# Expert chunks of a two-expert router: rows sent to one list, handed on to the other list, stored once

## The chip, the cores and the metric

The kernel runs on one core of a Trainium2 chip. The metric is the device time of one execution in microseconds (us); before the change three timed runs gave 500.67, 501.40 and 501.75, median 501.4. A core has TensorE (PE; its weight loads are shown apart as PEld), VectorE (DVE), ScalarE (ACT), GpSimd (POOL) and SyncE (SP), which run their own instruction streams and meet at semaphores, and 16 DMA engines that they share.

## The reference

3125 tokens (graph nodes) of 256 numbers pass one layer:

```python
xn = _layernorm(x)
x = x + _L0_gnn_ref(xn, src, dst, ...) + _L0_mix_ref(xn[None], ...)[0]
x = x + _L0_ffn_ref(_layernorm(x)[None], ...)[0]

# _L0_ffn_ref, with tokens = _layernorm(x), 8 experts, the best 2 of each token:
rw, re = jax.lax.top_k(softmax(tokens @ router_w.T), 2)
rw = rw / rw.sum(-1, keepdims=True)
combine = zeros((N, E)).at[arange(N)[:, None], re].set(rw)
out = tokens
for e in range(8):
    y = gelu(tokens @ w1[e] + b1[e]) @ w2[e] + b2[e]
    out = out + combine[:, e:e + 1] * y
```

The first line's two terms are a graph network over 53125 edges and a linear attention. The change lies in the last one. For these inputs the best expert (rank 0) is chosen by 248, 448, 389, 253, 479, 398, 435 and 475 tokens, the second (rank 1) by 270, 403, 411, 291, 488, 389, 433 and 440. In chunks of 128 rows of one expert that makes 28 chunks of rank 0 and 30 of rank 1.

## The kernel before

The graph and attention stages run until about 280 us. Tokens lie 125 to a partition in 25 tiles, `rows[125, 25, ROW]`; a row holds the 256 normalized numbers (`xb`) and 5 more: the token's number, the weights of rank 0 and rank 1, and the spread and mean with which the un-normalized value is restored.

*Routing.* The 25 tiles are taken in six groups (`ROUT`: 2, 5, 5, 5, 5, 3 tiles). For a group ScalarE normalizes, TensorE transposes and makes the logits, VectorE picks the two experts (`choose`), weighs and works out the place of each token in the lists (`weigh`, line 1051). `slot_i` (line 1067) holds for each token two row numbers in the DRAM tensor `xs`: one in the list of its rank 0 expert, one in that of its rank 1 expert. `xs` has two halves of RR rows, one for each rank. When a group's slots are there, GpSimd sends its rows to the rank 0 lists, one indirect DMA a tile (`send`, line 543: 125 rows of 1044 bytes). Rank 1 sends of earlier tiles are put between: one behind each of the groups 0 to 4, eight behind group 5 (BETWEEN, EARLY), and the last 12 between the chunks.

*The chunk table.* VectorE counts the lists and makes a table of 2 x 32 chunks (lines 1087 to 1120): expert and first row of each. A list whose length isn't a multiple of 128 is filled at its front with null rows, and the chunks behind the last real one read null rows only. A null row has the token number NOWHERE, so that its scatter is out of bounds and moves nothing. The null rows are written early by SyncE: two large stores (line 357) and 16 small ones (line 392), one behind each of 16 transposing DMAs of the graph stage.

*The chunks.* Chunks 0 to 31 are rank 0, 32 to 63 rank 1, and all engines run through them as one loop. For each, SyncE loads 128 rows from `xs` into `xch` (six buffers; `load_chunk`, line 394; buffer c % 6 is free when VectorE has weighed chunk c - 6). TensorE transposes them (`turn_rows`), does the first layer (line 1466) and the second (lines 1475 and 1477); it runs `turn_rows(c+2)`, `first_layer(c+1)`, `second_layer(c)` in this order. ScalarE copies the transposed rows, does the gelu and, for rank 0, restores the un-normalized rows in place (`restore`, line 709). VectorE copies the expert's weights two chunks ahead (lines 1129, 1130) and then weighs (`weigh_rows`): for rank 0 weight x y + restored row (line 1142), for rank 1 weight x y (line 1145), into one of four buffers `ys`. GpSimd scatters `ys` to the tokens' rows of `out` (`add_rows`, line 555): rank 0 by a plain write, rank 1 by an accumulating one, behind a wait for all rank 0 writes. SyncE waits for the rank 0 sends before chunk 0 and for the rank 1 sends before chunk 32. Ahead of chunk 0 TensorE runs 20 matmuls that only keep it busy (`keep_clock`, line 1165).

## Time and profile before

| | |
|---|---|
| timed runs | 500.67, 501.40, 501.75 us; median 501.4 |
| span of the profiled execution, first to last instruction | 511.2 us |
| PE busy | 456.7 us, 89% of the span |
| DVE, ACT, POOL busy | 318.7, 288.5, 234.0 us |
| graph and attention | 0 to about 280 us |
| routing | about 280 to 344 us |
| chunks | 356 to 504 us |
| chain that ended last | PE 57%, POOL 11%, issue 11%, DMA 8%, DVE 6% |

The profiled execution has no time of its own beside its span; the span is 9.8 us longer than the median of the timed runs. Times of rows are us from the span's start. "Issue" is a wait for which the profile shows no cause. A group of matmuls shows the time from its first start to its last modelled end. A gap in square brackets is idle time of the engine ahead of the instruction, with what ended it.

### The profile page before, as it was taken

How to read it: one execution, taken by the hardware profiler on the slowest of the kernel's cores; microseconds unless marked ns; L12 is line 12 of the kernel's file. 1: busy time of each engine (PE TensorE's matmuls, PEld its weight loads, DVE VectorE, ACT ScalarE, POOL GpSimd, SP SyncE). 2: the span in 40 equal slices, each digit the busy share in tenths (PEclk: the TensorE clock that was granted, in tenths of full speed). 3: DMA queues.
4: the chain of work that ended last, by engine and by line, in shares of the span. 5: the costliest groups of instructions: out<-in, count | busy, mean ns of one | idle time of the engine just before them, and what ended most of it. 6: DMA issues, size and time to landing. Idle time of an engine off the chain costs nothing.

```text
span 511.2 us, 10298 instructions
## 1 busy us (share of the span) xinstructions
PE 456.7 (89%) x3383; PEld 341.3 (67%) x3383; DVE 318.7 (62%) x866; ACT 288.5 (56%) x657; POOL 234.0 (46%) x259
## 2 busy tenths in 40 slices
PE   2899999978999999999998999735979889999994
PEld 1788888855666665566554575522968778999993
DVE  3686658755777776777740898472356466666662
ACT  1775555556777776777761688500556556544441
POOL 5035865453111111111110027778557765688775
PEclk9999999997999999999998998767899999999999
DMA  8705310947667776677662012334434444367763
GB/s 219 171 3 166 84 24 4 316 96 144 150 149 150 151 150 151 151 150 130 130 134 60 3 32 77 83 89 116 129 105 136 132 122 123 74 112 119 115 109 36
DMA packets 122451, 58.73 MB, mean 115 GB/s; under 512 B 95797, under 2 KB 119585, under 8 KB 122398
## 3 DMA queue, kind: packets, MB, share of 16 engines
q1 hardware_dynamic: 107838, 42.83, 35.8%
q0 software_dynamic: 13744, 14.39, 13.2%
q10 hardware_dynamic: 816, 0.85, 0.7%
q8 instruction: 28, 0.46, 0.4%
q14 instruction: 25, 0.20, 0.1%
HBM read 19.14 MB, written 20.34 MB: 77 GB/s over the span
## 4 chain that ended last, share of the span: by engine, by line
PE 57%; POOL 11%; issue 11%; DMA 8%; DVE 6%; ACT 4%; SPq 1%; POOLq 1%; DVEq 0%; another core or an unknown queue 0%; ACTq 0%
PE bank L1265 11%; PE bank L1254 9%; POOL out L562 6%; PE bank L1466 6%; POOL xs L544 5%; PE bank L1477 4%; PE bank L1190 4%; DMA region_a<-region_a 4%; PE bank L1296 4%; PE bank L1200 3%; PE bank L1203 3%; DMA rows<-in_x 2%; PE bank L1165 2%; PE bank L1276 2%; PE bank L1455 1%
## 5 line engine op out<-in xcount | busy, mean ns | idle before, releaser
L628 ACT CAST region_a<-bank 128x500 bf16<-128x500 f32 (+1 forms) x175 | 111.6, 667 | 48.6 <-PE bank L1254 43.0
L544 POOL DMA_INDIRECT xs<-rows,slot_i x50 | 62.5, 1249 | 50.3 <-issue 45.1
L1265 PE MATMUL bank<-region_a,region_z 125*64 125x500 bf16 (+1 forms) x525 | 72.1, 371 | 3.2 <-DMA region_a<-region_a 3.2
L1466 PE MATMUL bank<-region_a,region_c 128*128 128x128 f32 x512 | 70.7, 282 | 4.8 <-ACT region_a L697 2.6
L1254 PEld LDWEIGHTS bank<-region_a 128*128 128x128 bf16 x625 | 41.2, 102 | 46.1 <-issue 32.0
L518 POOL COPY wide<-den 125x256 f32<-125x256 f32 x25 | 11.4, 455 | 127.3 <-DVE den L942 127.3
L1254 PE MATMUL bank<-region_a 128*128 128x125 bf16 x625 | 65.4, 223 | 4.0 <-ACT region_a L628 2.8
L1466 PEld LDWEIGHTS bank<-region_a,region_c 128*128 128x128 f32 x512 | 63.8, 196 | 7.3 <-issue 3.6
L1477 PE MATMUL bank<-region_c,region_a 128*128 128x256 f32 x256 | 66.1, 380 | 0.0
L705 ACT ACTIVATE region_a<-bank,region_c 128x128 f32<-128x128 f32 x128 | 40.2, 366 | 42.9 <-PE bank L1466 24.9
L562 POOL DMA_INDIRECT out<-region_a x32 | 53.1, 1661 | 14.3 <-issue 12.3
L1129 DVE COPY region_c<-region_w 128x1026 f32 x64 | 46.2, 722 | 20.5 <-issue 20.3
L697 ACT COPY region_a<-bank 128x256 f32<-128x256 f32 x64 | 23.9, 374 | 44.6 <-PE bank L1455 39.9
L1477 PEld LDWEIGHTS bank<-region_c,region_a 128*128 128x128 f32 x256 | 44.1, 192 | 4.2
L866 DVE TENSOR_TENSOR region_a<-iota,locs 128x3200 bf16<-128x3200 bf16 x25 | 46.2, 1848 | 0.0
L559 POOL DMA_INDIRECT out<-region_a x32 | 33.8, 1057 | 25.9 <-DVE region_a L1142 19.1
L860 DVE TENSOR_TENSOR region_a<-iota,keys 128x3150 bf16<-128x3150 bf16 x25 | 45.4, 1818 | 0.2 <-PE bank L1254 0.2
L1140 DVE CAST region_a<-region_a 128x1 int32<-128x1 f32 x64 | 9.9, 155 | 49.8 <-issue 32.6
L1265 PEld LDWEIGHTS bank<-region_a,region_z 125*64 125x64 bf16 x525 | 25.0, 111 | 23.3 <-DMA region_a<-region_a 3.9
L1165 PE MATMUL bank<-zeros,ones 128*128 128x512 bf16 x114 | 32.9, 437 | 6.8 <-DVE expert_i L1119 6.8
L467 POOL TENSOR_SCALAR rows<-rows,rstd,shift 125x256 f32<-125x256 f32 x25 | 18.2, 732 | 33.1 <-DVE region_a L753 33.0
L1190 PE MATMUL bank<-wzkv,region_a 128*125 128x320 f32 x100 | 32.3, 446 | 0.0
(219 smaller groups left out, 800.3 us busy)
## 6 DMA issues: line engine op xcount, KB each, us to landing
region_a<-xs SPq DMA_DIRECT2D x64, 130.5 KB
region_w<-in_w SPq DMA_DIRECT2D x4, 1024.0 KB, 9.4
rows<-in_x SPq DMA_DIRECT2D x5, 560.0 KB
xs<-null SPq DMA_DIRECT2D x16, 130.5 KB, 2.3
xs<-null SPq DMA_DIRECT2D x2, 913.5 KB, 7.7
ztab<-region_z SPq DMA_DIRECT2D x5, 234.4 KB
out<-region_a POOLq DMA_INDIRECT x64
xs<-rows,slot_i POOLq DMA_INDIRECT x50
```

The costliest lines, as they stand in the source:

```text
L544: nc.gpsimd.indirect_dma_start(xs, bass.IndirectOffsetOnAxis(slot_i[:, t, r2:r2 + 1], 0), rows[:, t, :], None).then_inc(sent[r2], 16)
L562: nc.gpsimd.indirect_dma_start(out, to, ys[:, c % 4, :], None, bounds_check=N - 1, oob_is_err=False, compute_op=ALU.add).then_inc(added[c ...
L628: nc.scalar.copy(to, chunk_ps[n % 2][:, 0:w * TP].rearrange("p (c t u) -> p c t u", c=w, t=NT)).then_inc(adj_done, 1)
L860: nc.vector.tensor_tensor(koh[:, t % 2, :, :].rearrange("p c (m u) -> p c m u", u=2), counting(KW), columns(keys, t, KW), ALU.is_equal).th ...
L866: nc.vector.tensor_tensor(loh[:, t % 2, :, :].rearrange("p c (m u) -> p c m u", u=2), counting(P), columns(locs, t, P), ALU.is_equal).then ...
L1129: nc.vector.tensor_copy(wc[:, c % 3, :].rearrange("p (a f) -> p a f", a=1), w_all[:, bass.ds(e, 1), :])
L1165: nc.tensor.matmul(ps[:], ones16[:], zeros[:], start=True, stop=True)
L1190: last = nc.tensor.matmul((y0, y1)[s][0:TP, 0:H1 + D], xnT[:, s, k, :], wzkv[:, k, 0:H1 + D], start=(k == 0), stop=(k == 1))
L1254: last = nc.tensor.matmul(chunk_ps[n % 2][:, (c - lo) * TP:(c - lo + 1) * TP], loh[:, t % 2, c, :], koh[:, t % 2, c, 0:TP], start=True, st ...
L1265: last = nc.tensor.matmul(block_out(b), zparts[:, t, part, :], adjT[0:TP, t % 2, lo:hi, 0:TP], start=False, stop=False, skip_group_check=True)
L1466: last = nc.tensor.matmul(hid_ps[c % 2][:, f * P:(f + 1) * P], wc[:, c % 3, k * D + f * P:k * D + (f + 1) * P], xT[:, c % 2, k * P:(k + 1) ...
L1477: last = nc.tensor.matmul(y_ps[c % 2][:, 0:D], hT[:, c % 2, f * P:(f + 1) * P], wc[:, c % 3, (2 + f) * D:(3 + f) * D], start=False, stop=( ...
```

## The change

A token's row is sent once, to its rank 0 list. It carries its row number in the rank 1 list as a sixth extra number (NEXT, from `slot_f`), so ROW is 262. `xs` has one half; a second DRAM tensor `xs_next` holds the rank 1 lists with rows of WIDE = ROW + 256 numbers (2072 bytes). A rank 0 chunk is loaded into the front part of a buffer of `xch` (now 8 buffers, WIDE each); ScalarE writes the restored row to the back part (PART), VectorE adds weight x y there, and GpSimd scatters the whole wide row to `xs_next` (`hand_on`). SyncE waits until all 32 of these scatters have landed, then loads rank 1 chunks with wide rows; VectorE adds weight x y to the part, and GpSimd writes it to `out` by a plain scatter (`write_rows`). A buffer is free when its scatter has landed (`added`). The loops of TensorE and ScalarE no longer run through the border between chunk 31 and 32, and TensorE runs 20 more `keep_clock` matmuls there. The null rows of `xs_next` are wide. The 25 rank 1 sends and the buffers `ys` are gone.

```diff
-ROW = D + 5
+ROW = D + 6
+PART, WIDE = ROW, ROW + D
+TOKEN, NEXT, W_A, W_B, SPAN, MEAN = range(D, D + 6)
...
-BETWEEN, EARLY = 1, 13
-XB = 6
+XB = 8
...
-    xs = nc.dram_tensor("xs", (2 * RR, ROW), F32, kind="Internal").ap()
+    xs = nc.dram_tensor("xs", (RR, ROW), F32, kind="Internal").ap()
+    xs_next = nc.dram_tensor("xs_next", (RR, WIDE), F32, kind="Internal").ap()
...
-            for r2 in range(2):
-                sp.dma_start(xs[r2 * RR + NX * CAP:(r2 + 1) * RR, :].rearrange("(b p) d -> p b d", p=P),
-                             null[:].rearrange("p (a d) -> p a d", a=1).to_broadcast([P, NULLS, ROW])
+            for to, w in ((xs, ROW), (xs_next, WIDE)):
+                sp.dma_start(to[NX * CAP:RR, :].rearrange("(b p) d -> p b d", p=P),
+                             null[:, 0:w].rearrange("p (a d) -> p a d", a=1).to_broadcast([P, NULLS, w])
                              ).then_inc(nulls_stored, 16)
...
                     r2, e = divmod(t - 2, NX)
-                    at = r2 * RR + e * CAP
-                    sp.dma_start(xs[at:at + P, :], null[:]).then_inc(nulls_stored, 16)
+                    to, w = ((xs, ROW), (xs_next, WIDE))[r2]
+                    sp.dma_start(to[e * CAP:e * CAP + P, :], null[:, 0:w]).then_inc(nulls_stored, 16)
...
                 if c >= XB:
-                    sp.wait_ge(ys_done, c - XB + 1)
-                sp.dma_start(xch[:, c % XB, :], xs[bass.ds(at, P), :]).then_inc(xch_in[c % XB], 16)
+                    sp.wait_ge(added[c % XB], c // XB * 16)
+                if c < MC:
+                    sp.dma_start(xch[:, c % XB, 0:ROW], xs[bass.ds(at, P), :]).then_inc(xch_in[c % XB], 16)
+                else:
+                    sp.dma_start(xch[:, c % XB, :], xs_next[bass.ds(at, P), :]).then_inc(xch_in[c % XB], 16)
...
-            sp.wait_ge(sent[0], NT * 16)
+            sp.wait_ge(sent, NT * 16)
             for c in range(NCH):
                 if c == MC:
-                    sp.wait_ge(sent[1], NT * 16)
+                    for s in range(XB):
+                        sp.wait_ge(added[s], len(range(s, MC, XB)) * 16)
                 load_chunk(c)
...
                 for t in range(lo, hi):
-                    send(t, 0)
-                for t in range(g * BETWEEN, (g + 1) * BETWEEN if g < NR - 1 else EARLY):
-                    send(t, 1)
+                    send(t)
...
+            def hand_on(c):
                 pool.wait_ge(ys_done, c + 1)
+                nc.gpsimd.indirect_dma_start(xs_next, bass.IndirectOffsetOnAxis(to_row[:, c:c + 1], 0),
+                                             xch[:, c % XB, :], None, bounds_check=RR - 1, oob_is_err=False
+                                             ).then_inc(added[c % XB], 16)
+
+            def write_rows(c):
+                pool.wait_ge(ys_done, c + 1)
+                nc.gpsimd.indirect_dma_start(out, bass.IndirectOffsetOnAxis(to_row[:, c:c + 1], 0),
+                                             xch[:, c % XB, PART:WIDE], None, bounds_check=N - 1, oob_is_err=False
+                                             ).then_inc(added[c % XB], 16)
...
-            copy_x(0)
-            for c in range(NCH):
-                if c + 1 < NCH:
-                    copy_x(c + 1)
+            for lo, hi in ((0, MC), (MC, NCH)):
+                copy_x(lo)
+                for c in range(lo, hi):
+                    if c + 1 < hi:
+                        copy_x(c + 1)
...
+                nc.vector.tensor_copy(rows[0:TP, lo:hi, NEXT], slot_f[:, 0:n, 1])
+                nc.vector.tensor_copy(slot_i[0:TP, lo:hi, :], slot_f[:, 0:n, 0:1]).then_inc(slot_done, 1)
...
+                goal, weight = (NEXT, W_A) if c < MC else (TOKEN, W_B)
+                nc.vector.tensor_copy(to_row[:, c:c + 1], xch[:, s, goal:goal + 1])
                 if c < MC:
                     dve.wait_ge(restored, c + 1)
+                nc.vector.scalar_tensor_tensor(xch[:, s, PART:WIDE], y_ps[c % 2][:, 0:D], xch[:, s, weight:weight + 1],
+                                               xch[:, s, PART:WIDE], ALU.mult, ALU.add).then_inc(ys_done, 1)
...
-            turn_rows(0)
-            turn_rows(1)
-            first_layer(0)
-            for c in range(NCH):
+            for lo, hi in ((0, MC), (MC, NCH)):
+                if lo == MC:
+                    keep_clock(lg_ps, 20)
+                turn_rows(lo)
+                turn_rows(lo + 1)
+                first_layer(lo)
+                for c in range(lo, hi):
```

## Rows read from the trace of the kernel before

**Rows 1.** Timeline of VectorE: start us, us, instruction; last slots of group 4, table ready.

```profile
333.17 0.17 DVE L1067 CAST slot_i<-slot_f 125x10 int32<-125x10 f32 x1
...
343.38 0.17 DVE L1119 TENSOR_SCALAR expert_i<-expert_f 1x64 int32<-1x64 f32 x1
```

**Rows 2.** Chain that ended last, in order of time: start us, us, what.

```profile
346.67 4.75 DMA xs<-rows,slot_i
...
352.54 3.62 DMA region_a<-xs
...
439.08 2.09 DMA out<-region_a
```

**Rows 3.** Timeline of TensorE: warming matmuls, first layers of chunks 0 and 2.

```profile
316.41 1.90 PE L1165 MATMUL bank<-zeros,ones 128*128 128x512 bf16 x8
...
343.70 6.90 PE L1165 MATMUL bank<-zeros,ones 128*128 128x512 bf16 x20 [6.75 <-DVE expert_i L1119]
...
357.36 2.08 PE L1466 MATMUL bank<-region_a,region_c 128*128 128x128 f32 x8
...
363.02 1.06 PE L1466 MATMUL bank<-region_a,region_c 128*128 128x128 f32 x8
```

**Rows 4.** Timeline of VectorE: weighing of chunks 0, 31, 62 and 63.

```profile
363.13 0.47 DVE L1142 SCALAR_TENSOR_TENSOR region_a<-bank,region_a 128x256 f32<-128x256 f32 x1
...
437.81 0.48 DVE L1142 SCALAR_TENSOR_TENSOR region_a<-bank,region_a 128x256 f32<-128x256 f32 x1
...
501.01 0.48 DVE L1145 TENSOR_SCALAR region_a<-bank,region_a 128x256 f32<-128x256 f32 x1
...
503.85 0.48 DVE L1145 TENSOR_SCALAR region_a<-bank,region_a 128x256 f32<-128x256 f32 x1
```

**Rows 5.** Windows: us; PE PEld DVE ACT POOL busy; PEclk, DMA share, GB/s.

```profile
400.00:410.00 10.00, 8.01 (x52) 6.56 (x51) 4.76 (x16) 5.47 (x16) 6.51 (x7) 1.00 0.39 117
...
460.00:470.00 10.00, 10.00 (x73) 9.13 (x72) 6.51 (x20) 4.94 (x15) 8.23 (x6) 1.00 0.68 116
```

**Rows 6.** Waits, 356 to 441 us: total us, times, longest.

```profile
PE bank L1466 <- ACT region_a L697: 2.6, 2, 1.9
PE bank L1466 <- issue: 2.2, 3, 1.2
PE bank L1475 <- ACT region_a L705: 1.9, 3, 1.2
```

**Rows 7.** GpSimd: two timeline rows, and three of lines (ns min/median/max, first, last start).

```profile
337.37 1.19 POOL L544 DMA_INDIRECT xs<-rows,slot_i  x1 [0.30 <-issue]
...
364.45 1.02 POOL L559 DMA_INDIRECT out<-region_a  x1 [4.13 <-DVE region_a L1142]
...
L562 POOL DMA_INDIRECT out<-region_a x32: 1547/1596/2049, 442.1 to 506.0; - x32
...
L487 POOL DMA_INDIRECT region_c<-in_dst,row_i x5: 1207/1211/1646, 50.0 to 56.5; - x5
...
L494 POOL DMA_INDIRECT region_w<-codes,start_i x5: 1209/1212/1458, 68.1 to 74.4; - x5
```

**Rows 8.** Windows around changes of TensorE's granted clock (the third number from the end).

```profile
320.00:323.50 3.50, 0.77 (x5) 0.15 (x3) 1.51 (x9) 1.01 (x3) 2.58 (x4) 1.00 0.32 91
...
325.50:331.00 5.50, 5.50 (x20) 3.37 (x20) 2.85 (x27) 3.08 (x5) 4.58 (x4) 0.50 0.29 78
...
352.00:355.00 3.00, 0.00 (x0) 0.00 (x0) 0.00 (x0) 0.00 (x0) 2.39 (x3) 1.00 0.52 116
...
357.00:359.00 2.00, 1.96 (x9) 1.64 (x8) 0.00 (x0) 1.93 (x3) 1.52 (x2) 0.50 0.77 202
```

**Rows 9.** DMA issues by line: number, KB each, median us from issue to landing.

```profile
xs<-null SPq DMA_DIRECT2D x16, 130.5 KB, 2.3
xs<-null SPq DMA_DIRECT2D x2, 913.5 KB, 7.7
```

**Rows 10.** Waits, 105 to 285 us (graph stage): total us, times, longest.

```profile
PE bank L1265 <- DMA region_a<-region_a: 3.2, 3, 2.0
```

More of the change, by code:

```diff
@@ L47 @@
 RR = NX * CAP + NULLS * P
-NOWHERE = 4096.0
+NOWHERE = 65536.0
 CTX0 = 128
@@ L124, in build @@
         r.restart()
+        xch = r.take(P, XB * WIDE).rearrange("p (s d) -> p s d", s=XB)
+        r.restart()
         h1T = r.take(P, (HALF_TILES + 1) * TP)
@@ L194, in build @@
         base = sb("base", [TP, 2 * NX])
-        null = sb("null", [P, ROW])
+        null = sb("null", [P, WIDE])
         b2own = sb("b2own", [P, NX * D // P])
@@ L294, in build @@
             "slot_done", "cum_done", "cnt_ready", "table_done"))
-        sent = [sem(f"sent{r2}") for r2 in range(2)]
+        sent = sem("sent")
         xch_in = [sem(f"xch_in{s}") for s in range(XB)]
-        added = [sem(f"added{s}") for s in range(4)]
+        added = [sem(f"added{s}") for s in range(XB)]
         xt_ready, xT_done, w_copied, hid_ready, gelu_done, y_ready, ys_done = map(sem, (
@@ L421, in _ @@
             nc.gpsimd.memset(null[:, 0:D], 0.0)
+            nc.gpsimd.memset(null[:, ROW:WIDE], 0.0)
             nc.gpsimd.memset(null[:, D:ROW], NOWHERE).then_inc(null_set, 1)
@@ L541, in _, with send @@
                 pool.wait_ge(wins_landed[b], 16)
-            def send(t, r2):
-                nc.gpsimd.indirect_dma_start(xs, bass.IndirectOffsetOnAxis(slot_i[:, t, r2:r2 + 1], 0),
-                                             rows[:, t, :], None).then_inc(sent[r2], 16)
+            def send(t):
+                nc.gpsimd.indirect_dma_start(xs, bass.IndirectOffsetOnAxis(slot_i[:, t, 0:1], 0),
+                                             rows[:, t, :], None).then_inc(sent, 16)
             for g, (lo, hi) in enumerate(ROUT):
@@ L550, in _ @@
                 for t in range(lo, hi):
[L551 to L555 removed]
+                    send(t)
+            def hand_on(c):
                 pool.wait_ge(ys_done, c + 1)
[L557 to L571 removed]
+                nc.gpsimd.indirect_dma_start(xs_next, bass.IndirectOffsetOnAxis(to_row[:, c:c + 1], 0),
[6 more added lines that the diff above has]
+                                             ).then_inc(added[c % XB], 16)
+            for c in range(MC):
+                hand_on(c)
+            for c in range(MC, NCH):
+                write_rows(c)
         @block.scalar
@@ L1485, in _ @@
             keep_clock(m0, 20)
[L1486 to L1494 removed]
+            for lo, hi in ((0, MC), (MC, NCH)):
[5 more added lines that the diff above has]
+                for c in range(lo, hi):
+                    if c + 2 < hi:
+                        turn_rows(c + 2)
+                    if c + 1 < hi:
+                        first_layer(c + 1)
+                    second_layer(c)
 def kernel(**inputs):
```

64 lines of the change are left out of this document (16 added, 48 removed).

## The prediction

> **What bounds the kernel now.** I read the windows first, to see which engine is full in which stage; then the chain of waits in order of time, to see what starts the expert stage and what ends it; then the timelines of VectorE, GpSimd and TensorE at the two ends of that stage, where each wait can be put down to one instruction. The change touches three places: the end of the routing stage, the border between the rank 0 and the rank 1 chunks, and the end of the kernel. It also makes rows of one list twice as long.
>
> *Start of the expert stage.* VectorE has the chunk table ready at 343.55 and the slots of token group 4 at 333.34, but GpSimd starts the last rank 0 send only at 346.67 [rows 1, 2]. The chain then reads: 4.75 us from that send to its landing at 351.42, 1.12 us of SyncE to the first load's issue at 352.54, and 3.62 us for that load, after which TensorE transposes from 356.2 on [rows 2]. So sends set the start. TensorE's own 20 warming matmuls are over at 350.60, 5.6 us earlier [rows 3].
>
> *Rank 0 and rank 1 chunks.* VectorE's weighing of a chunk tells the pace: the first ends at 363.60, the last of rank 0 starts at 437.81, the last of rank 1 at 503.85 [rows 4]. Rank 1 runs at (503.85 - 437.81)/32 = 2.06 us a chunk with TensorE busy all the time [rows 5]: TensorE bounds it. Rank 0 runs at (437.81 - 363.13)/31 = 2.41 us, so it loses 0.35 x 31 = 10.7 us to something; 6.7 us of it stand as idle TensorE in the table of waits [rows 6]. There is no break between the two halves: TensorE already works on chunks 32 and 33 while GpSimd waits for the last rank 0 stores.
>
> *End.* The last weighing is over at 504.33, GpSimd's last accumulating scatter starts at 506.0 and is over at 507.5, because each takes 1.6 us and they are late by then [rows 7], and the span ends at 511.2: 6.87 us of tail.
>
> **The change, part by part.**
>
> *Fewer sends before the start.* 13 of the 38 sends ahead of the first chunk go, but only those queued before the last rank 0 send count. The other 8 stand behind it. After the change GpSimd has no backlog when the slots of group 4 come at 333.34: 8 sends at 1.49 us (1.19 and 0.30 idle before it [rows 7]) follow, and the last starts at 333.55 + 7 x 1.49 = 343.98 instead of 346.67. Gain 2.7 us. Next late is the load itself (353.5), then the warming matmuls (350.60). If the routing stage's own waits are shorter in an execution without profiler, the four interleaved rank 1 sends count in full, 6.0 us, cut to 5.6 by the warming matmuls. TensorE would then stand idle for 2.8 us, not 5.6. In the trace of before it starts the chunks at half clock (0.50), 1.2 GHz, while from 352 to 355, idle, it still was granted 1.00, 2.4 GHz; after a stretch of 3.5 us with 0.77 us of work it fell to 0.50 too [rows 8]. A kept clock would save some 2.2 us of the first chunks (a first layer took 2.08 us there and 1.06 us later [rows 3], and two of them and the transposes stand before the first weighing). I take half of it, 1.1. Together **-3.8** (bounds -7.8 and -2.7).
>
> *The pace of the rank 0 chunks.* The 12 sends between chunks go, the store is a scatter of 2072 bytes a row in place of 1024, and buffers are freed by its landing rather than by VectorE. TensorE, ScalarE and VectorE have the same instructions of the same sizes: VectorE's copy of the goal only moves ahead of a wait. GpSimd's cost of a scatter: the rows show 1.19 us for 125 rows of 1044 bytes, 1.02 for 128 rows of 1024, and, for gathers, 1.21 both for rows of 1700 bytes (L487) and of 512 (L494) [rows 7], so it doesn't go by bytes, and I take 1.2 us and 0.3 of issue: well under 2.06. Moved bytes: 131 + 259 KB a chunk, 193 GB/s at that pace; the DMA engines moved 202 GB/s at 0.77 busy when the loads began [rows 8], so they hold. The ring of eight buffers: load c+8 waits for the landing of scatter c. From the weighing's end GpSimd needs 0.85 us to start (363.60 to 364.45 [rows 4, 7]); the landing takes 2.09 us after that for a scatter without data and 4.75 for a send in the crowd [rows 2]; 128 KB more is 0.9 us, from the two sizes of null stores, (7.7 - 2.3)/(913.5 - 130.5) us a KB [rows 9]; SyncE 0.4; the load 2.3 (a store of that size, rows 9) to 3.62. That is 6.5 to 10.5 us. It has five chunks less 0.65 us, 9.7 us. I take about 8, near the quiet rows, and **0**; the upper end is (10.5 + 0.65)/5 = 2.23 us a chunk, 3.8 us over the 24 chunks that wait so; the lower end is a gain of all 10.7 us that rank 0 now loses (first rival).
>
> *The hand-over.* This is the new wait. SyncE waits for all 32 hand-ons, so nothing of chunk 32 can be loaded, and loads, transposes and both layers, which now run through the border, start anew. From the end E of the last rank 0 weighing: 0.85 to GpSimd's start, 2.09 to the landing (rank 0 fills 28 chunks, so the last four scatter nothing, and that row is such a one), 1.1 for SyncE, 3.2 for the load (2.3 + 0.9 for the wider row), and then the start-up of the pipeline, which took from 356.2 to 363.60 at half clock, 7.4 us [rows 2, 4]: E + 14.6. Without the border the next weighing would end at E + 2.07. Back comes what TensorE no longer does ahead at the end of rank 0, as at the end of rank 1, where the last two intervals are 2.84 us together (501.01 to 503.85 [rows 4]) instead of 4.13: -1.3. Sum **+11.2**. The 20 added matmuls take some 4.5 us at full clock (eight took 1.90 [rows 3]) and fit between E - 0.6, when TensorE is done, and E + 7.2, when the load has landed; they leave 3.3 us idle, close to the stretch after which the clock fell [rows 8], so I take the half clock. Bounds: with the clock kept 2.2 less, 9.0; with a load of 3.62 + 0.9, 12.5.
>
> The Trainium skill, "DMA: Bandwidth & Descriptors", section "Anatomy of one DMA — SWDGE (gpsimd) path", gives a DMA some 2.0 us fixed and its bytes at 436 GB/s. The trace agrees for the fixed part (2.09 us for the scatter without data). By that rule, read for SyncE's loads too, the wide load would be an estimated 2.6 us and the forecast 0.6 us lower.
>
> *The rank 1 chunks.* Loads of 259 KB, stores of 128 KB without the accumulation: GpSimd falls from 1.6 to 1.0 us a chunk. TensorE bounded it and still does: **0**. The ring: 0.85 + 2.1 to 4.75 + 0.4 + 3.2 to 4.5 = 6.6 to 10.5 us against 9.7, so 0 to +3.8 again.
>
> *The tail.* GpSimd is no longer late: start 0.85 us after the last weighing, 1.02 us, and 3.7 us as now from its last instruction to the end: 5.6 instead of 6.87. **-1.3** (the bound is 0, if the landing of the last loads and stores ends it).
>
> *Before the routing.* One of the two big null stores grows to 1813 KB, eight of the sixteen small ones to 259 KB. The big ones go out at 41 to 42 us; at the rate of rows 9 the extra 900 KB are 6.2 us, so they would be done near 56 and meet the gathers of L487, whose readers on VectorE don't wait today and have about 3 us before them. The small ones stand in SyncE's queue behind a transpose of 3.8 us in a period of 6.3 us; TensorE waits for transposes three times, 3.2 us [rows 10]. I take **+0.3** (bounds 0 and 2). The extra memset of null (0.3 us) lies under the first loads of x.
>
> **Sum.** -3.8 + 0 + 11.2 + 0 - 1.3 + 0.3 = **+6.4 us**, on an execution whose span was 511.2 us. The timed runs have a median of 501.4, 9.8 us less than that span: part of the waits of the profiled execution (the rank 0 ones, I suspect) is not in them. All my terms but one come from places where the work is bound by one chain, so I carry the difference over as it is: 501.4 + 6.4 = **507.8 us**.
>
> **The rivals.** *1, the other side: rank 0 speeds up.* Its lost 10.7 us could come from GpSimd's and the DMA queues' work on the 12 interleaved sends. For it: TensorE is idle for 2.0 of the 10 us from 400 on, where sends are, and not at all in rank 1 [rows 5]. Against it: rank 1 has more DMA work (0.68 busy against 0.39 [rows 5]), a busier GpSimd, and no stall; and the timed runs may not have these stalls at all. It decides from 6.4 us given back, 60% of the loss; all of it gives 507.8 - 10.7 = 497.1 us. Chance 0.18, of which 0.13 faster by over 0.2% and 0.05 about equal.
> *2, the ring is too small.* Landings near the slow row for both halves: 507.8 + 7.6 = 515.4 us. Chance 0.12.
> *3, GpSimd's scatter goes by bytes.* 2 x 1.02 + 0.3 = 2.32 us a chunk in rank 0, 0.26 x 28 = 7.3: 515.1 us. Chance 0.04.
> *4, the border is nearly free,* that is, the change doesn't serialize as it says, because landing, load and start-up overlap better than the rows show (hand-over 5 to 6 us): about 502. Chance 0.04, half within 0.2%.
> The forecast itself has 0.62, with its own range from -5.6 + 9.0 - 1.3 = +2.1 to -2.7 + 12.5 + 0.6: 503.5 to 512.
>
> **Numbers.** Within 0.2% (1 us) is about what a measurement of this kernel can't tell from no change. Faster 0.13, within 0.07, slower 0.80. The range takes in the second and third rival and the middle of the first: 500.0 to 515.5.
>
> **What would show it.** Right: in the changed kernel's VectorE timeline a gap of 12 to 15 us between the last weighing of rank 0 and the first of rank 1; the first transpose of the chunks near 353; rank 1 at 2.06 us a chunk; a tail near 5.5 us. Wrong: a rank 0 pace under 2.2 us (rival 1), TensorE waiting for loads inside either half (rival 2), scatters over 2 us on GpSimd (rival 3), or TensorE waiting for transposes in the graph stage more than three times.

## The result, and the profile after

The changed kernel takes 505.74 us, median of six runs (504.08 to 508.9), against 501.03 us for the kernel before (six runs, 500.24 to 502.11). The ratio is 1.0094, with a 95% interval of 1.0068 to 1.012. The forecast was 507.8 us, slower. In all comparisons fast runs stand against fast ones: three runs of the kernel before, two on chip A and one on chip D below, took over 1.5% more than its fastest there and are left out.

The profiled execution took 505.36 us, with a span of 503.6 us. The page's busy times and its chain read:

```profile
PE 454.9 (90%) x3403; PEld 339.5 (67%) x3403; DVE 316.5 (63%) x872; ACT 289.5 (57%) x657; POOL 179.9 (36%) x235
...
PE 72%; DMA 11%; ACT 5%; DVE 3%; issue 3%; POOL 3%; SPq 1%; POOLq 0%; DVEq 0%; ACTq 0%
```

GpSimd has lost 54 us of its 234; the time didn't fall. Of the chain, TensorE holds 72% (57% before), DMA 11% and GpSimd 3% (11% before).

The trace of before that stands ahead of the prediction (span 511.2 us) is no partner for this one: it is longer than any timed run of before beside it. A later execution of the same kernel before, called g0 below, was timed at 501.36 us with a span of 499.6 us, on a chip where before has a median of 501.88. The comparison goes by that one, though it isn't from the chip of the changed kernel's trace. Its VectorE timeline shows the weighing of chunks 0, 31 and 63, the rows that answer to [rows 4]:

```profile
360.95 0.47 DVE L1142 SCALAR_TENSOR_TENSOR region_a<-bank,region_a 128x256 f32<-128x256 f32 x1
...
426.32 0.48 DVE L1142 SCALAR_TENSOR_TENSOR region_a<-bank,region_a 128x256 f32<-128x256 f32 x1
...
492.28 0.47 DVE L1145 TENSOR_SCALAR region_a<-bank,region_a 128x256 f32<-128x256 f32 x1
```

VectorE of the changed kernel, chunks 0, 31, 32 and 63:

```profile
354.11 0.47 DVE L1146 SCALAR_TENSOR_TENSOR region_a<-bank,region_a 128x256 f32<-128x256 f32 x1
...
418.17 0.47 DVE L1146 SCALAR_TENSOR_TENSOR region_a<-bank,region_a 128x256 f32<-128x256 f32 x1
...
431.81 0.47 DVE L1146 SCALAR_TENSOR_TENSOR region_a<-bank,region_a 128x256 f32<-128x256 f32 x1
...
495.55 0.47 DVE L1146 SCALAR_TENSOR_TENSOR region_a<-bank,region_a 128x256 f32<-128x256 f32 x1
```

Between these marks (ends of the weighings, in us) the span splits into five stretches. All kernels below are read in the same way:

| stretch | before (first trace) | before (g0) | changed | changed less g0 |
|---|---|---|---|---|
| start to the end of chunk 0 | 363.60 | 361.42 | 354.59 | -6.8 |
| rank 0, chunks 0 to 31 | 74.68 | 65.38 | 64.05 | -1.3 |
| border, chunk 31 to 32 | 2.18 | 2.19 | 13.64 | +11.45 |
| rank 1, chunks 32 to 63 | 63.86 | 63.76 | 63.74 | 0.0 |
| tail | 6.87 | 6.87 | 7.61 | +0.7 |
| span | 511.2 | 499.6 | 503.6 | +4.0 |

The medians differ by 4.7 us, the two traces by 4.0.

*The start.* The changed kernel's chain has, in order of time, the last send, the load of chunk 1, the last rank 0 scatter, SyncE's issue of the load of chunk 32, and the load of chunk 33:

```profile
341.46 4.09 DMA xs<-rows,slot_i
...
347.79 2.11 DMA region_a<-xs
...
419.44 2.05 DMA xs_next<-region_a
...
422.32 0.34 SPq L403
...
423.42 3.12 DMA region_a<-xs_next
```

The last send starts at 341.46 us (345.66 in g0, 346.67 in [rows 2]), and the load takes 2.11 us rather than 2.93 in g0's chain (3.62 in [rows 2]). The first transpose follows at 348.82 (353.76 in g0, 4.9 us). VectorE casts the last group's slots before that, in g0 and then in the changed kernel:

```profile
331.78 0.17 DVE L1067 CAST slot_i<-slot_f 125x6 int32<-125x6 f32 x1
...
333.28 0.16 DVE L1073 CAST slot_i<-slot_f 125x3 int32<-125x3 f32 x1
```

The last send starts 13.9 us behind that cast in g0 and 8.2 us behind it in the changed kernel: GpSimd's queue of sends is 5.7 us shorter, and the cast itself is 1.5 us later. The other 1.9 us of the gain is mostly TensorE's clock: the start-up from that transpose to the first weighing takes 5.77 us against 7.66. The windows of the changed kernel, with its warming matmuls, the idle stretch behind them and the start-up, show it (the third number from the end is the granted clock):

```profile
342.00:345.00 3.00, 3.00 (x9) 1.08 (x8) 0.97 (x2) 0.00 (x0) 0.94 (x1) 0.50 0.27 76
345.00:348.00 3.00, 1.73 (x8) 0.59 (x6) 0.00 (x0) 0.00 (x0) 0.00 (x0) 0.97 0.09 28
349.00:354.00 5.00, 3.92 (x30) 3.35 (x30) 0.00 (x0) 3.92 (x10) 0.00 (x0) 1.00 0.50 130
```

TensorE stood idle for 2.1 us and kept the upper level, 2.4 GHz. In g0 it stood idle for 9.03 us and started at half, 1.2 GHz:

```profile
354.00:359.00 5.00, 4.36 (x21) 3.96 (x21) 0.00 (x0) 3.40 (x7) 3.90 (x4) 0.50 0.68 179
```

One pair of traces can't give the start to better than some 2 us. VectorE's first cast of slots (`slot_i`), which stands ahead of all sends, starts at 295.83 us in g0 and at 297.74 in the changed kernel. Over all fourteen traces it starts anywhere from 294.87 to 299.34, on average at 296.6 in the eight of before's form and at 296.8 in the six of the changed form. Pairs from one chip, in the table at the end of the experiments, give -7.3 us (g2 against g0), -5.3 (a0 against e5) and -6.7 (e6 against e5).

*Rank 0 and rank 1.* The windows of the changed kernel and of g0, in each the second half of rank 0 and then rank 1 (the answer to [rows 5]):

```profile
390.00:417.00 27.00, 27.00 (x192) 24.64 (x192) 17.87 (x53) 18.62 (x51) 13.09 (x13) 1.00 0.46 147
434.00:490.00 56.00, 56.00 (x402) 51.44 (x402) 37.03 (x107) 26.84 (x81) 26.92 (x28) 1.00 0.57 166
```

```profile
390.00:426.00 36.00, 36.00 (x258) 32.98 (x257) 25.48 (x70) 25.45 (x69) 24.32 (x24) 1.00 0.47 136
434.00:490.00 56.00, 56.00 (x402) 51.32 (x401) 37.13 (x108) 26.30 (x80) 44.33 (x28) 1.00 0.68 111
```

TensorE is busy without a pause in all four, so it bounds both halves, at 2.066 and 2.056 us a chunk in the changed kernel. The rank 0 stalls of the first trace of before aren't in g0.

*The border.* TensorE of the changed kernel: its 20 warming matmuls, then the transposes of chunk 32 behind their load, then the two first layers of the start-up:

```profile
417.27 4.48 PE L1166 MATMUL bank<-zeros,ones 128*128 128x512 bf16 x20
...
425.14 0.44 PE L1456 MATMUL bank<-ident,region_a 128*128 128x128 f32 x2 [3.38 <-DMA region_a<-xs_next]
...
426.85 1.70 PE L1467 MATMUL bank<-region_a,region_c 128*128 128x128 f32 x8
...
428.78 1.88 PE L1467 MATMUL bank<-region_a,region_c 128*128 128x128 f32 x8
```

The last weighing of rank 0 ends at 418.64, the last scatter starts at 419.44 and has landed at 421.49, SyncE issues the load of chunk 32 at 422.32, its rows are transposed from 425.14 on (those of chunk 33 land at 426.54), and the first rank 1 weighing is over at 432.28. The first layers take 1.70 and 1.88 us where they take 1.06 at the full clock [rows 3].

*The tail.* GpSimd's last store starts 1.10 us behind the last weighing and is over at 498.09:

```profile
497.12 0.97 POOL L568 DMA_INDIRECT out<-region_a  x1 [0.30 <-issue]
```

Behind it GpSimd's queue has only a drain of any length, and the other engines wait for its end (its row starts 0.5 us ahead of the store's). The row gives its duration in ns (min/median/max), then its first and last start:

```profile
L59 POOLq DRAIN  x1: 6809/6809/6809, 496.6 to 496.6; - x1
```

It ends at 503.4 us, 5.3 us after the store. In g0 it is over 3.4 us after the last store:

```profile
L57 POOLq DRAIN  x1: 6086/6086/6086, 493.3 to 493.3; - x1
```

SyncE has its last landing at 499.3 us in the changed kernel, so no transfer sets the end: GpSimd's drain does.

### The profile page after: what moved, and what is told of

Read it like the earlier page. It is cut to its first block, busy times and chain, and to the rows that moved or that the text cites. A ratio compares the mean times of both kernels' runs of the same rounds, so it can differ in the third digit from the quotient of the medians.

```text
span 503.6 us, 10296 instructions
## 1 busy us (share of the span) xinstructions
PE 454.9 (90%) x3403; PEld 339.5 (67%) x3403; DVE 316.5 (63%) x872; ACT 289.5 (57%) x657; POOL 179.9 (36%) x235
## 4 chain that ended last, share of the span: by engine, by line
PE 72%; DMA 11%; ACT 5%; DVE 3%; issue 3%; POOL 3%; SPq 1%; POOLq 0%; DVEq 0%; ACTq 0%
PE bank L1467 11%; PE bank L1266 11%; PE bank L1478 11%; PE bank L1255 8%; DMA region_a<-region_a 6%; PE bank L1297 4%; PE bank L1191 4%; PE bank L1166 3%; PE bank L1201 3%; PE bank L1204 3%; PE bank L1456 3%; DMA rows<-in_x 2%; PE bank L1404 2%; PE bank L1277 1%; PE bank L1476 1%
## 5 line engine op out<-in xcount | busy, mean ns | idle before, releaser
L1467 PE MATMUL bank<-region_a,region_c 128*128 128x128 f32 x512 | 69.4, 279 | 0.0
L1135 DVE COPY region_c<-region_w 128x1026 f32 x64 | 44.7, 699 | 17.0 <-issue 16.1
L568 POOL DMA_INDIRECT out<-region_a x32 | 32.3, 1010 | 45.4 <-DVE region_a L1146 42.8
L562 POOL DMA_INDIRECT xs_next<-region_a x32 | 32.1, 1003 | 45.4 <-DVE region_a L1146 44.1
L551 POOL DMA_INDIRECT xs<-rows,slot_i x25 | 30.5, 1219 | 44.5 <-issue 37.4
L1166 PE MATMUL bank<-zeros,ones 128*128 128x512 bf16 x134 | 36.9, 425 | 6.9 <-DVE expert_i L1125 6.9
L1456 PE MATMUL bank<-ident,region_a 128*128 128x128 f32 x128 | 24.9, 276 | 7.2 <-DMA region_a<-xs_next 4.4
```

Of the source, the lines that this page charges most:

```text
L1135: nc.vector.tensor_copy(wc[:, c % 3, :].rearrange("p (a f) -> p a f", a=1), w_all[:, bass.ds(e, 1), :])
L1166: nc.tensor.matmul(ps[:], ones16[:], zeros[:], start=True, stop=True)
L1456: last = nc.tensor.transpose(xt_ps[c % 2][:, k * P:(k + 1) * P], xch[:, c % XB, k * P:(k + 1) * P], ident[:])
L1467: last = nc.tensor.matmul(hid_ps[c % 2][:, f * P:(f + 1) * P], wc[:, c % 3, k * D + f * P:k * D + (f + 1) * P], xT[:, c % 2, k * P:(k + 1) ...
```

## The experiments

They ran on four chips, called A to D, each with the kernel before beside them. The chips differ: before takes 511.86 us on A (median of 9 runs), 501.15 on B (25), 501.88 on C (23) and 509.26 on D (16). Each ratio is to before on its own chip. A table of all stretches stands after the last experiment.

**e0, the kernel before again (chip A).**

> The kernel before, unchanged, profiled a second time. Theory A: the rank 0 stalls of the first trace (rank 0 at 2.41 us a chunk, 10.7 us lost, span 511.2) belong to that one execution and are not in the timed runs of 501 us. Then this trace has a span of 499 to 501 us, rank 0 at 2.07 to 2.12 us a chunk and the first weighing's end some 4 to 6 us earlier than 363.6. Theory B: the stalls come from the sends between the chunks and are in every execution: rank 0 again at 2.3 us a chunk or more.

515.12 us, span 513.3. Rank 0 takes 73.3 us there, as in the first trace of before (74.7) and unlike g0 (65.4). Windows within rank 0, and waits from 360 to 443 us (total us, times, longest):

```profile
368.00:390.00 22.00, 20.31 (x139) 17.82 (x138) 13.14 (x38) 13.27 (x39) 15.00 (x14) 1.00 0.44 126
390.00:440.00 50.00, 46.34 (x319) 40.78 (x318) 29.58 (x84) 29.94 (x84) 32.73 (x30) 1.00 0.44 124
```

```profile
ACT region_a L705 <- remote: 4.2, 2, 2.3
...
PE bank L1466 <- issue: 2.6, 5, 0.6
```

TensorE is busy for 66.7 of 72 us. Of its waits behind the start of the chunks 3.9 us are "issue", and 1.2 are for ScalarE. ScalarE's own waits "remote" are those for whose end the profile names no instruction at all. They stand in the first trace of before (8.5 us of ScalarE's in the list of waits of [rows 6]) and in all four traces of chip A (e0 to e3), and in none of the nine others.

The stalls aren't in rank 0 alone. The last cast of slots in e0, and in e2, the changed kernel without its border, on the same chip:

```profile
341.19 0.17 DVE L1067 CAST slot_i<-slot_f 125x6 int32<-125x6 f32 x1
```

```profile
338.87 0.26 DVE L1072 CAST slot_i<-slot_f 125x3 int32<-125x3 f32 x1
```

They come 9.4 us later than in g0 and 5.6 later than in the changed kernel's trace, with "remote" waits of ScalarE and VectorE before them (4.9 and 3.9 us in e0, 2.4 of ScalarE's in e2). Of the 13.7 us between the spans of e0 and g0, 1.8 stand ahead of the first cast of slots, 4.1 between it and the first weighing, and 7.9 in rank 0. So the stalls of the first trace are a property of an execution on some chips, not of the kernel alone.

**e1, the border put into before (chip A).** SyncE waits for all rank 0 stores before chunk 32, and the loops break there; all else is as before.

```diff
                 if c == MC:
+                    for s in range(4):
+                        sp.wait_ge(added[s], MC // 4 * 16)
...
-            turn_rows(0)
-            turn_rows(1)
-            first_layer(0)
-            for c in range(NCH):
+            for lo, hi in ((0, MC), (MC, NCH)):
+                if lo == MC:
+                    keep_clock(lg_ps, 20)
+                turn_rows(lo)
+                turn_rows(lo + 1)
+                first_layer(lo)
+                for c in range(lo, hi):
```

> The kernel before with the border of the change alone: SyncE waits for all rank 0 stores before it loads chunk 32, the loops of TensorE and ScalarE break there, and TensorE runs 20 more matmuls. Lists, row lengths and sends as before. Theory: the hand-over costs 10 to 11 us wherever it stands (10.8 us between the two weighings of the changed kernel, less 0.4 to 0.8 because this load is 131 KB and not 259): 501.0 + 10 = 510 to 512.5 us. Rival: it costs that much only because of the wide rows and their landing, and here 6 to 7 us: 507 to 508 us.

522.38 us, ratio 1.0186 (1.0117 to 1.0254), that is some 9.5 us more. VectorE's weighing of chunks 31 and 32:

```profile
441.40 0.48 DVE L1145 SCALAR_TENSOR_TENSOR region_a<-bank,region_a 128x256 f32<-128x256 f32 x1
...
453.93 0.48 DVE L1148 TENSOR_SCALAR region_a<-bank,region_a 128x256 f32<-128x256 f32 x1
```

12.53 us between the weighings instead of 2.18: the border costs 10.35 us with narrow rows, 1.1 us less than with wide ones, and some 9.9 where the last two intervals of rank 0, 3.76 us together instead of 4.17 in e0, are set against it. It is the cost of the change, and it comes alone.

**e2, the changed kernel without the border (chip A).** The loops run through. Rank 1 chunks are loaded from a block of null rows with the same bytes, so rank 1's sums are left out and `out` is not written.

```diff
-                    sp.dma_start(xch[:, c % XB, :], xs_next[bass.ds(at, P), :]).then_inc(xch_in[c % XB], 16)
+                    sp.dma_start(xch[:, c % XB, :], xs_null).then_inc(xch_in[c % XB], 16)
...
-                if c == MC:
-                    for s in range(XB):
-                        sp.wait_ge(added[s], len(range(s, MC, XB)) * 16)
```

> The changed kernel without the border: the loops run through, and rank 1 chunks are loaded, 259 KB each, from a block of null rows stored early instead of from the rank 1 lists, so that nothing waits for the hand-ons. Left out: the rank 1 results, and the stores to out move nothing. Theory: the border is the loss, so this is 505.7 - 10.8 = 494 to 496 us, that is 5 to 7 us faster than the kernel before, which is what fewer sends before the start give. Rival: the wide loads and scatters cost something of their own beside TensorE: 498 us or more.

500.58 us, ratio 0.9736 (0.9674 to 0.9797). Rank 0 takes 64.83 us on the chip on which e0 takes 73.31 and e1 76.57:

```profile
360.00:424.00 64.00, 64.00 (x460) 58.89 (x460) 42.31 (x123) 45.26 (x123) 31.05 (x31) 1.00 0.55 170
```

64 of 64 us busy. So everything in the change but the border is a gain there, and the rank 0 stalls of chip A go with what the change takes out of rank 0. Those of the routing stage stay, and chunk 0 is over at 360.09 us, 5.5 later than in the changed kernel's trace. Its tail is 7.61 us, as in the changed kernel.

**e3, five rank 1 sends moved behind the rank 0 sends, in before (chip A).** `BETWEEN, EARLY = 0, 13`: the start comes earlier, and nothing else changes.

```diff
-BETWEEN, EARLY = 1, 13
+BETWEEN, EARLY = 0, 13
```

> The kernel before with the five rank 1 sends that stand between the routing groups moved behind the last group (BETWEEN 0 instead of 1; as many sends before the first chunk as before). Theory: sends ahead of the last rank 0 send set the start of the chunks, four or five of them at 1.49 us each count until the warming matmuls bind: 4 to 6 us faster than before, 495 to 497 us, and the first load's landing near 350. Rival: the routing engines set the start, as the first trace shows it in part: 2.7 us or less, 498 to 500 us.

514.41 us, ratio 1.0037 (0.9979 to 1.0095). Against e0 chunk 0 is over 8.7 us earlier (358.60), of which 4.6 stand already in the last slots (336.64), whose work the edit doesn't touch; but rank 0 takes 79.86 us, 6.6 more, and TensorE is busy for 32.5 of the 40 us from 352 to 392.

An earlier start is not worth its size while the sends are only moved.

**a0, the changed kernel itself, on chip B.**

> The changed kernel itself, unchanged, on the chip of this study. On such a chip the kernel before took 514 us (rank 0 at 2.37 us a chunk in its second trace), against 501 where the result was measured. Theory: the changed kernel has no rank 0 stalls on either chip (2.07 to 2.09 us a chunk, as with the border taken out: 500.6 us), so here it takes 500.6 + 10.8 = 510 to 512 us and is equal to or faster than the kernel before if that is at 514. Rival: the stalls are the chip's and hit both: some 520 us, slower than before by as much as in the result.

506.64 us, ratio 1.0094 (1.0058 to 1.013), the same as the first measurement.

**e4, before without the 12 sends between the chunks (chip B).** The rank 1 chunks read null rows, so rank 1's part of the sum is left out.

```diff
-                if c % 2 == 0 and c // 2 + EARLY < NT:
-                    send(c // 2 + EARLY, 1)
```

> The kernel before without the 12 rank 1 sends between the rank 0 chunks. Left out: those sends, and the rank 1 chunks load null rows, so the rank 1 half of the result is missing and its stores move nothing. Theory: the sends between chunks cause the rank 0 stalls: 2.07 to 2.10 us a chunk and 8 to 11 us less than before. Rival: ring, stores or code cause them: 2.3 us a chunk or more, within 2 us of before.

502.81 us, ratio 1.0035 (1.0004 to 1.0066). Rank 0 takes 64.83 us, the least of the kernels of this form, 0.55 less than g0, and the same as the changed form has in e2. The tail grows to 9.43 us.

**e5, before with those 12 sends moving nothing (chip B).** They are issued as before, but every index is out of bounds. Rank 1 is left out as in e4.

```diff
-                    send(c // 2 + EARLY, 1)
+                    nc.gpsimd.indirect_dma_start(xs, bass.IndirectOffsetOnAxis(far[0:TP, 0:1], 0),
+                                                 rows[:, c // 2 + EARLY, :], None, bounds_check=N - 1, oob_is_err=False
+                                                 ).then_inc(sent[1], 16)
```

> As the run without sends between, but the 12 sends are issued with row numbers that are all out of bounds: GpSimd works through each, and no row is moved. Left out: the rank 1 half, as there. If GpSimd's time on the sends is the cause (1.02 + 0.3 a store and half of 1.49 a send make 2.07 us a chunk, all of TensorE's pace): 2.3 us a chunk or more and near before's time. If the rows' traffic in the DMA engines is the cause: 2.07 to 2.12 us a chunk and 8 to 11 us less than before.

502.08 us, ratio 1.0014 (0.9985 to 1.0042); rank 0 takes 65.26 us. Against g0's 65.38 us (from chip C) neither the sends' bytes nor their issue costs rank 0 more than some 0.5 us where before takes 501: rival 1's gain is not there to be had.

**e6, the changed kernel with 12 sends put back (chip B).** Into a tensor that nobody reads.

```diff
+                if c % 2 == 0 and c // 2 + 13 < NT:
+                    nc.gpsimd.indirect_dma_start(xs_copy, bass.IndirectOffsetOnAxis(slot_i[:, c // 2 + 13, 0:1], 0),
+                                                 rows[:, c // 2 + 13, :], None).then_inc(sent_again, 16)
```

> The changed kernel with 12 sends put between its rank 0 chunks as in the kernel before, of the same rows to a DRAM tensor that nobody reads; the result stays whole. If sends between chunks cause the stalls: rank 0 goes from 2.07 to 2.3 to 2.5 us a chunk, 7 to 12 us more than the changed kernel itself. If the stalls came from anything else of the kernel before: within 2 us of the changed kernel.

510.63 us, ratio 1.0179 (1.0137 to 1.022), 4.0 us more than a0. Rank 0 takes 67.14 us instead of 64.06, the border 0.65 more (SyncE waits there for these sends too), the tail 1.0 more. GpSimd's timeline in rank 0:

```profile
369.88 1.35 POOL L578 DMA_INDIRECT xs_copy<-rows,slot_i  x1 [0.30 <-DVE region_a L1152]
371.54 0.99 POOL L565 DMA_INDIRECT xs_next<-region_a  x1 [0.30 <-issue]
372.84 1.05 POOL L565 DMA_INDIRECT xs_next<-region_a  x1 [0.31 <-issue]
```

One send and two scatters with their gaps are 1.65 + 1.29 + 1.36 = 4.3 us for two chunks, 2.15 a chunk, and the rank 0 pace is 2.166: here GpSimd bounds it.

**g0, the kernel before again (chip C).** The partner of the table above.

> The kernel before, unchanged, for a third trace. On the first chip of this study it took 514 us with rank 0 at 2.37 us a chunk, on the second 501. Theory: the rank 0 stalls are what tells the two apart. On a chip that times it at 501, rank 0 runs at 2.07 to 2.12 us a chunk and the span is 499 to 500; on one that times it at 514, at 2.3 or more. Rival: the 13 us lie elsewhere (the graph stage, the start), and the rank 0 pace is 2.3 on both.

501.36 us. Its GpSimd timeline at the end of the stretch that has sends:

```profile
408.83 1.05 POOL L559 DMA_INDIRECT out<-region_a  x1 [0.30 <-issue]
410.19 1.20 POOL L544 DMA_INDIRECT xs<-rows,slot_i  x1 [0.30 <-DVE region_a L1142]
411.69 0.99 POOL L559 DMA_INDIRECT out<-region_a  x1 [0.30 <-issue]
412.99 1.05 POOL L559 DMA_INDIRECT out<-region_a  x1 [0.30 <-issue]
...
417.16 0.99 POOL L559 DMA_INDIRECT out<-region_a  x1 [1.08 <-DVE region_a L1142]
```

Two chunks with their send take 412.99 - 408.83 = 4.16 us, 2.08 a chunk, where TensorE takes 2.06. The gaps are 0.30 us until the sends are through, and 1.08 us only after them. GpSimd is full in rank 0, level with TensorE, though its share of the span is 46%.

**g1, e3's edit again (chip C).**

> The kernel before with its five rank 1 sends between the routing groups moved behind the last group, again. On the first chip the first weighing came 5 to 9 us earlier and rank 0 lost it again (2.58 us a chunk): no gain. Theory: where rank 0 has no stalls nothing takes the gain back, 496 to 498 us on a chip where the kernel before takes 501; on one where it takes 514, equal again. Rival: GpSimd, at 1.0 + 0.3 a store and half of 1.5 a send, is full during rank 0 in either case and takes it back on every chip: within 1 us of before.

502.01 us, ratio 1.0025 (0.9989 to 1.0061). Chunk 0 is over at 358.03, 3.4 us before g0, but GpSimd's first store starts 5.9 us behind it (0.85 in g0), because sends stand in the way, and rank 0 takes 70.15 us, 4.8 more. GpSimd has 12 sends and 24 stores within the first 24 chunks, 12 x 1.5 + 24 x 1.3 = 49.2 us against TensorE's 24 x 2.06 = 49.4; five more sends are 7.5 us for which it has no room, and rank 0 pays for what the start has gained. VectorE then waits for the buffers of the stores:

```profile
DVE region_a L1140 <- DMA out<-region_a: 2.2, 2, 2.0
```

**g2, the changed kernel with 34 warming matmuls at the border (chip C).** SyncE also fetches the row number of chunk 32 ahead of the waits.

```diff
-                if c >= XB:
+                if c == MC:
+                    for s in range(XB):
+                        sp.wait_ge(added[s], len(range(s, MC, XB)) * 16)
+                elif c >= XB:
...
-                if c == MC:
-                    for s in range(XB):
-                        sp.wait_ge(added[s], len(range(s, MC, XB)) * 16)
...
-                    keep_clock(lg_ps, 20)
+                    keep_clock(lg_ps, 34)
```

> The changed kernel with 34 instead of 20 matmuls at the border, and with SyncE's read of the row number ahead of its wait for the hand-ons instead of behind it. Theory: TensorE stays at full clock through the start of rank 1 (7.1 us from the first transpose to the first weighing become 5 to 5.7) and the load goes out 0.6 us earlier: border 11.3 us instead of 13.6, 2 to 2.8 us less than the changed kernel, so ratio to before about 1.004 where that of the change is 1.009. Rival: the clock isn't kept, or doesn't matter: 0.6 us or less.

505.03 us, ratio 1.0062 (1.0037 to 1.0087). TensorE at the border:

```profile
416.98 7.29 PE L1166 MATMUL bank<-zeros,ones 128*128 128x512 bf16 x33
424.10 0.38 PE L1456 MATMUL bank<-ident,region_a 128*128 128x128 f32 x2
...
425.64 1.06 PE L1467 MATMUL bank<-region_a,region_c 128*128 128x128 f32 x8
```

No idle time ahead of the first transposes (0.88 us behind them), a first layer of 1.06 us, and a start-up of 5.4 us instead of 7.1. The border is 11.33 us, 2.3 less: 1.8 by the kept clock and 0.5 by the earlier fetch. It is the best whole form of the changed kernel that ran, and it still loses to before on this chip. Its trace is of the fastest of its 12 runs, 2.5 us under their median, so the spans of g2 and g0 lie closer together than the medians.

**h1, the changed kernel again (chip D).**

> The changed kernel once more, beside the kernel before on whatever chip this is. Theory: the changed kernel takes 504 to 507 us on every chip, because nothing of it stalls in rank 0; what varies is the kernel before. So on a chip where that takes 501 the ratio is again 1.006 to 1.012, and on one where it takes 514 the changed kernel is 1 to 2% faster. Rival: a slow chip slows both alike, and the ratio is 1.009 everywhere.

507.78 us, ratio 0.9972 (0.9938 to 1.0006). Where before takes 509.26 us, the change costs nothing that can be told from noise. The changed kernel has medians of 505.74, 506.64 and 507.78 us in its three measurements; before has 501 to 512.

**All stretches**, in us, from one profiled execution each:

| kernel (chip) | to chunk 0 | rank 0 | border | rank 1 | tail | span |
|---|---|---|---|---|---|---|
| e0 before (A) | 367.26 | 73.31 | 2.18 | 63.68 | 6.87 | 513.3 |
| e1 border in before (A) | 365.31 | 76.57 | 12.53 | 63.66 | 6.87 | 524.9 |
| e2 changed, no border (A) | 360.09 | 64.83 | 2.09 | 63.74 | 7.61 | 498.4 |
| e3 sends behind (A) | 358.60 | 79.86 | 2.18 | 63.80 | 6.88 | 511.3 |
| a0 changed (B) | 356.37 | 64.06 | 13.56 | 63.75 | 7.61 | 505.4 |
| e4 no sends between (B) | 362.88 | 64.83 | 2.19 | 63.48 | 9.43 | 502.8 |
| e5 sends without data (B) | 361.67 | 65.26 | 2.19 | 63.48 | 7.19 | 499.8 |
| e6 changed, with sends (B) | 355.00 | 67.14 | 14.21 | 63.74 | 8.59 | 508.7 |
| g0 before (C) | 361.42 | 65.38 | 2.19 | 63.76 | 6.87 | 499.6 |
| g1 sends behind (C) | 358.03 | 70.15 | 2.18 | 63.78 | 6.88 | 501.0 |
| g2 changed, 34 matmuls (C) | 354.08 | 64.05 | 11.33 | 63.74 | 7.61 | 500.8 |
| h1 changed (D) | 354.52 | 64.05 | 13.90 | 63.74 | 7.61 | 503.8 |

## Why the prediction was right, term by term

The forecast was 507.8 us, the result 505.7, and what makes it slower is what was named: the border. Two errors of opposite sign lie in the sum, one of -3.0 us at the start and one of +2.0 in the tail; the other terms are 1.4 us below their forecast together (null stores 0.3, rank 0 pace 0.6, hand-over 0.5). In all +4.0 where +6.4 was forecast. That the two errors nearly cancel is luck.

*Start, -3.8 forecast, -6.8 measured.* Right in kind: the sends set it, and the clock is kept after a short idle stretch. The step that failed is the choice between "2.7 us" and "the four interleaved rank 1 sends count in full". The 2.7 rest on slots of group 4 at 333.34, in a trace whose routing stage had stalls; they were there at 328.1 in g0 and 329.3 in the changed kernel, so that GpSimd's queue counted for 5.7 us, near that second bound of 6.0, and these slots' and the last group's coming 1.2 to 1.5 us later took some of it back. The last send starts 4.2 us earlier than in g0, and send and load behind it are 0.7 us shorter. The clock gave up to 1.9 us where I took half of 2.2. The measured value lies within the bounds. The forecast's own range used -5.6 for its lower end; with the start's own bound of -7.8 it would have begun at 501.3 and not at 503.5.

*Rank 0 pace, 0 forecast, -0.6 measured* (of the table's -1.3, 0.74 belong to the hand-over's lookahead; e4, before without the sends, has the same 0.55 less). The suspicion that the stalls of the first trace aren't in the timed runs was right: g0, timed like the median, has 65.38 us where that trace has 74.68. The argument that GpSimd was "well under" TensorE's pace was right for the changed kernel only, at 1.0 us for a scatter of 2072 bytes:

```profile
L562 POOL DMA_INDIRECT xs_next<-region_a x32 | 32.1, 1003 | 45.4 <-DVE region_a L1146 44.1 <-issue 1.3
```

I never summed GpSimd for rank 0 of the kernel before. It was full there, as g0 and g1 show, and e6 makes it full again in the changed kernel. That term has a second side: the gain at the start is kept only because the 12 sends left rank 0 as well. Moved and not removed (g1, e3), 3.4 and 8.7 us at the start came to nothing.

*Hand-over, +11.2 forecast, +10.7 measured.* From the last weighing's end: 0.80 us to GpSimd's start (0.85 forecast), 2.05 to the landing (2.09), 0.83 for SyncE (1.1), 2.82 for the load (3.2) and 7.14 for the start-up (7.4), together 13.64 where 14.6 was forecast. 2.19 go off for an ordinary interval. The lookahead that comes back at the end of rank 0 is smaller than the 1.3 forecast: its last two intervals are 3.40 us instead of 4.14, so 0.74. The clock did fall: g2 kept it, and 1.8 of the 2.3 us that it gained are of that. e1 shows the border alone, +10.35 us between the weighings.

*Rank 1 pace, 0 forecast, 0.0 measured.* TensorE bounds it. GpSimd fell from 44.3 to 26.9 us of 56, and it bought nothing.

*Tail, -1.3 forecast, +0.7 measured.* The step that failed is "3.7 us as now from its last instruction to the end", carried over from the kernel before. It is 5.5 us in the changed kernel. Even so the store starts 1.10 and not 0.85 us after the last weighing. The end is GpSimd's drain, and its length was read as if it were the landing of the last stores. Its length is one of a kernel, not of an execution: from the last scatter's end it is 3.4 to 3.5 us in all traces of before and in e1, e3, g1 and e5, 5.3 in those of the changed kernel and in e2 and g2, 5.6 in e4 and 6.3 in e6. What sets it isn't settled: it is longer with 99 indirect DMAs than with 124, but e4 has 112 and e6 has 111, and no run varied it alone.

*Null stores, +0.3 forecast.* TensorE's waits for transposes in the graph stage, the answer to [rows 10]:

```profile
PE bank L1266 <- DMA region_a<-region_a: 3.7, 4, 1.9
```

0.5 us more, at four places instead of three, but that is no mark of the change: e3 and e5, which store no wide null rows, have four such waits too (4.7 and 4.3 us), g2 has two (2.4 us), and the first cast of slots comes no later in the changed kernel than in before. The term can't be told from nothing, and the sign of being wrong that was set down for it, more than three such waits, came true without meaning anything.

*Rival 1* (rank 0 gets its lost time back; 497.1 us) is false where before takes 501 us, by e4 and e5, and half true on chip A. There the rank 0 stalls appear only in kernels that have sends between the chunks (73.3 us in e0, 76.6 in e1, 79.9 in e3), and not in the changed form without them (64.8 in e2), which differs from before in more than the sends. On chip D rank 0 may have regained what the border cost, for the kernels are equal; no trace of before was taken on D, so that is argued from A's traces and not shown. The rival's size was right for the first trace; my weight against it rested on which execution the timed runs resemble. The sign set down for it, a rank 0 pace under 2.2 us, came true (2.066) without the rival's being so: it compares with the stalled trace's 2.41, while before itself runs at 2.11 in g0.

*Rival 2* (the ring too small; 515.4 us) is false: within the halves no load is waited for. The waits of TensorE for loads lie at the two starts alone:

```profile
PE bank L1456 <- DMA region_a<-xs_next: 4.4, 2, 3.4
...
PE bank L1456 <- DMA region_a<-xs: 2.8, 2, 2.1
```

*Rival 3* (scatter by bytes; 515.1) is false by the 1003 ns above for twice the bytes. Its sum was off by a little: 2 x 1.02 + 0.3 is 2.34 and not 2.32, which makes it some 515.6 us. *Rival 4* (border nearly free; 502) is false by 13.64 us.

Of the signs of being right, the gap (13.64 us between the weighings' ends) and the rank 1 pace came true; the first transpose at 348.8 us instead of "near 353" and the tail of 7.6 instead of 5.5 didn't.

**What stays open.** Which property of the chip makes the stalls in routing and rank 0, what stands behind the "remote" waits that go with them, and whether GpSimd's issue or the DMA traffic of the sends calls them up: e4 and e5 tell these two apart, but they ran only on chip B, where there are no stalls. And what sets the drain's length.

## What to carry to other kernels

A new dependence of a whole second half on a whole first half costs the drain of the last item (store, landing, notice, load) and the fill of the pipeline, here 10 to 11 us, whatever work is saved elsewhere; the saved work counts only where its engine set the pace. Sum each engine over the stage, not over the span: GpSimd had 46% of the span and was full in the stage next to TensorE, so that moving its work moved the time from one stretch to the next, and only removing it gave any. Before carrying terms to a time, look whether the profiled execution has the length of the timed ones, and if it hasn't, take none of its stalls as given.

## What the runs showed of the hardware that was not expected

- The same program took 501.0 to 501.9 us on some chips and 509.3 and 511.9 on two others, on the one that was traced (e0) with stalls in the routing stage and in rank 0, none in rank 1, and with waits marked "remote" that no trace of the two faster chips has, nor that of the changed kernel on D. The changed kernel took 505.7 to 507.8 us in three measurements, two beside a before of 501 us and one beside 509.3. Whether this change costs anything hangs on the chip.
- TensorE kept the granted clock of 1.00 (2.4 GHz) over 2.1 us without work at the start of the chunks. At the border it was granted 1.00 while idle (422 to 425 us) and 0.72 on average from 425 to 431, after 3.38 us of waiting, 0.44 us of transposes and another wait for rows:

```profile
422.00:425.00 3.00, 0.00 (x0) 0.00 (x0) 0.00 (x0) 0.00 (x0) 0.00 (x0) 1.00 0.46 102
425.00:431.00 6.00, 4.86 (x25) 4.54 (x26) 0.00 (x0) 1.94 (x7) 0.00 (x0) 0.72 0.79 227
```

- An indirect scatter of 128 rows takes GpSimd 1.0 us for 1024 and for 2072 bytes a row alike.
- A load of 259 KB took 3.0 us from issue to landing and one of 131 KB 2.4 (medians of 32). The Trainium skill, "DMA: Bandwidth & Descriptors", section "Anatomy of one DMA — SWDGE (gpsimd) path", read for SyncE's loads too, would give an estimated 2.6 and 2.3 by its fixed 2.0 us and 436 GB/s, so the trace lies 0.4 and 0.1 us above it. Its fixed part agrees with the 2.05 us of the scatter that moves nothing.

```profile
region_a<-xs_next SPq DMA_DIRECT2D x32, 259.0 KB, 3.0
...
region_a<-xs SPq DMA_DIRECT2D x32, 131.0 KB, 2.4
```
